# A graph network on one core: the share of node blocks that PE and POOL serve in its edge layer, and how edge weights reach the messages

## The chip, the cores and the metric

One core of a Trainium2 chip runs the whole network as one program. Times are device microseconds. The kernel before took 4041.06 us, the median of three runs (4039.64 to 4046.97).

## What is computed

There are 6250 nodes with 64 features and 200000 edges, sorted by destination. Four layers follow one another, each as x = layernorm(x + layer(x)).

```python
# layer 0: mean of the neighbours, one matrix over [h, mean]
# layer 1: twice: h = norm * segment_sum((h * norm)[src] * w, dst); mean of the three h
# layer 2: a message for every edge
x = jnp.concatenate([h[src], h[dst], e], axis=1)
m = jax.nn.relu(x @ W1 + b1) @ W2 + b2
h_new = jax.ops.segment_sum(m, dst, num_segments=h.shape[0])
# layer 3: two rounds of mean aggregation with matrices 64 -> 128 -> 64
```

Layer 2, the edge layer, is the one that cannot be done by a matrix of counts, since a relu stands on each edge. Its input splits into P[src] + Q[dst] + e * w, where P and Q are products per node (Q with b1 added) and w is the last row of W1.

## The kernel before

**Nodes and stages.** The nodes lie in 50 blocks of 125, in 10 groups of five. The stages: bounds of every node's edges are counted, with a histogram of edges by pair of blocks (`histogram`, L1672, on DVE, 34 batches of 46 columns); the 50 block matrices of counts and of weights are built and stored to DRAM (PE L1287, ScalarE L1041), with layer 0's dense sums inside (L1260); the node steps of layer 0; two weights passes for layer 1 (`weights_pass`, L1A and L1B); the edge layer (L2); two passes of layer 3 (L1328).

**Weights passes.** For each of the five blocks of a group, SP loads a matrix of 3125 KB (L697, three buffers; block 3 and block 4 of a group reuse those of blocks 0 and 1), and PE multiplies it in 100 matmuls (L1333), called a dense block below. Beside it the edges of the blocks that PE serves in the edge layer are sorted by source block. One sort: `sort_runs` on DVE (keys and one-hot comparisons), `sort_base` on PE (17 matmuls, L1428), `sort_ranks` on DVE (L2135 to L2147), then `sort_half` twice, DVE's product (L2154, L2160) and then 33 matmuls on PE (L1438), which gather local node number, local destination and three bf16 pieces of the edge weight into slots; ScalarE stores the halves to `sorted_edges`. PE, DVE and ScalarE take these steps in a written order between the dense blocks: one sort per group, the bases after dense block 0, the halves after dense blocks 3 and 4. In the second pass DVE also ends layer 1 for the group before (`finish`), and `dst_half` (L2053) makes Q.

**Edge layer.** Each group of five blocks has two served by PE (the last two) and three by POOL. The unit of order is a chunk: a block of POOL's has 33 columns of 128 edges and three chunks of 11. For each chunk:

- POOL gathers P rows by 11 indirect DMAs into one of four buffers (`gather_runs`, L931); a buffer is free when PE has collected the chunk four before.
- DVE compares the broadcast local destinations with the node numbers (`hot`, L2214, one in three chunks), PE spreads Q onto the edges (`spread`, L1475, 33 matmuls), DVE multiplies e by w (L2223) and adds PE's result from PSUM (L2227), makes the slot matrix (`slots_of`, L2234) and adds all to the gathered rows (`arrive`, L2241); ScalarE takes the relu (L1176); PE collects into the sums by destination (L1480).
- PE's own blocks, 100 slots of 128 sorted edges a group, go along in portions called units: SP broadcasts node and destination keys over 128 partitions into two tiles and then loads the three rows of edge weights (`load_unit`, L766); DVE makes one-hot matrices (L2193, L2194); PE multiplies them with the split P and Q (L1510, L1513, six matmuls a slot); ScalarE takes the relu (L1153); DVE makes slot matrices (L2205) in parts of up to six slots; PE collects (L1480).

All queues are in order. The DVE loop (L2248 and on) takes hot, unit hots, the Q half, unit slots, slots, arrive for each chunk. `split` (L556) cuts an f32 tile into three bf16 pieces: three casts and two subtractions with drains between them. At the start of the edge layer DVE splits P and then Q for all nodes.

## Time and profile before

| | |
|---|---|
| median of three runs | 4041.06 us |
| profiled execution | 4037.8 us, its span 4035.9 us |
| mean granted TensorE clock | 0.880 |
| busy: PE, DVE, ACT, POOL | 2965.3, 2213.4, 937.2, 1393.3 us |
| gathers of the edge layer (L931) | 990, 1091.0 us busy, mean 1102 ns |
| HBM read and written | 634.20 and 250.86 MB |

Busy is the time in which an engine had an instruction running. A wait is put down to the engine or transfer whose signal came last. PEclk is the clock that PE was granted, as a share of 2.4 GHz. The chain of waits follows the execution back from its end; the engines on it set the time.

### The profile page before, as it was taken

The page shows a single profiled execution, that of the slowest core. Times are in us where ns is not written, and L with a number is a line of the kernel's source. Part 1 is how long each engine was busy: PE and PEld are TensorE (multiplying, and loading weights), DVE is VectorE, ACT ScalarE, POOL GpSimd, SP SyncE. Part 2 cuts the span into 40 slices and gives each one's busy share as a digit, 9 for nine tenths or more (in the row PEclk, how much of TensorE's full clock was granted, in tenths as well). Part 3 has the DMA queues.
Part 4 walks back from the last instruction along what each step waited for, and adds up shares of the span by engine and source line. Part 5 has one row for each costly group of instructions (what it writes and reads, how often), then busy time and mean ns, then how long its engine had stood idle before and what let it go on. Part 6 is the DMA issues. An engine that isn't in the chain of part 4 may idle for free.

```text
span 4035.9 us, 119777 instructions
## 1 busy us (share of the span) xinstructions
PE 2965.3 (73%) x52730; PEld 2823.6 (70%) x52730; DVE 2213.4 (55%) x3076; ACT 937.2 (23%) x1994; POOL 1393.3 (35%) x1262
## 2 busy tenths in 40 slices
PE   0636999999995888888984655655555556489898
PEld 0635999999994878888874544555545555489898
DVE  8955777677766554455656555555545555411122
ACT  0004777777771000000000111111111111100000
POOL 5478100000000000000007777777777777600100
PEclk9999999999995999999996777777777777799999
DMA  4414787777884999999974333343333333287797
GB/s 122 83 35 128 272 289 286 269 284 273 287 288 163 402 403 391 403 391 404 400 325 114 93 92 99 99 109 92 91 100 97 104 97 99 69 346 288 261 380 312
DMA packets 334176, 891.87 MB, mean 221 GB/s; under 512 B 124164, under 2 KB 199032, under 8 KB 304088
## 3 DMA queue, kind: packets, MB, share of 16 engines
q1 hardware_dynamic: 279400, 835.28, 55.9%
q0 software_dynamic: 44480, 47.34, 5.6%
q8 instruction: 389, 6.37, 0.6%
q10 hardware_dynamic: 9792, 1.93, 0.3%
q14 instruction: 115, 0.94, 0.1%
HBM read 634.20 MB, written 250.86 MB: 219 GB/s over the span
## 4 chain that ended last, share of the span: by engine, by line
PE 32%; POOL 28%; issue 16%; DMA 15%; DVE 5%; ACT 1%; SPq 1%; POOLq 1%; DVEq 1%; ACTq 0%
POOL stream L931 27%; DMA stream<-a_weights 13%; PE ps L1287 13%; PE ps L1333 6%; PE ps L1260 5%; PE ps L1328 5%; POOL stream L909 1%; DVE junk L1615 1%; DMA a_counts<-stream 1%; ACT stream L1041 1%; DVE junk L1693 1%; DVE stream L1678 1%; PE ps L1394 1%; PE ps L1228 1%; SPq L675 0%
## 5 line engine op out<-in xcount | busy, mean ns | idle before, releaser
L931 POOL DMA_INDIRECT stream<-table,stream x990 | 1091.0, 1102 | 1998.9 <-DMA stream<-dst_run 1697.3
L1287 PE MATMUL ps<-operand_room 64*128 64x50 bf16 (+1 forms) x18750 | 635.1, 221 | 17.3 <-DVE operand_room L1860 8.0
L1475 PE MATMUL ps<-edge_room,stream 125*128 125x64 bf16 x2970 | 196.2, 242 | 609.5 <-DVE stream L2227 581.3
L1287 PEld LDWEIGHTS ps<-operand_room 64*128 64x128 bf16 x18750 | 613.8, 163 | 42.5 <-DVE operand_room L1860 8.5
L1333 PE MATMUL ps<-stream,node_room 125*64 125x125 f32 x10000 | 565.0, 273 | 92.8 <-DMA stream<-a_weights 85.6
L1475 PEld LDWEIGHTS ps<-edge_room,stream 125*128 125x128 bf16 x2970 | 185.4, 162 | 619.4 <-DVE stream L2227 416.8
L1333 PEld LDWEIGHTS ps<-stream,node_room 125*64 125x64 f32 x10000 | 542.0, 137 | 108.1 <-DMA stream<-a_weights 98.3
L1041 ACT CAST stream<-ps 128x500 bf16<-128x500 f32 (+2 forms) x700 | 431.3, 633 | 194.3 <-PE ps L1287 155.1
L1041 ACT COPY stream<-ps 128x500 f32<-128x500 f32 (+2 forms) x700 | 422.1, 619 | 0.0
L1328 PE MATMUL ps<-operand_room,stream 125*125 125x192 bf16 x3750 | 326.8, 250 | 4.4 <-POOLq L567 4.4
L1328 PEld LDWEIGHTS ps<-operand_room,stream 125*125 125x125 bf16 x3750 | 321.8, 140 | 4.6 <-POOLq L567 4.6
L2234 DVE TENSOR_TENSOR stream<-slot_f,stream 128x1375 f32<-128x1375 f32 x90 | 143.5, 1595 | 275.4 <-PE ps L1480 265.4
L1153 ACT ACTIVATE node_room<-ps 128x384 f32<-128x384 f32 (+1 forms) x180 | 83.5, 464 | 891.1 <-PE ps L1513 882.6
L1860 DVE TENSOR_TENSOR operand_room<-operand_room,node_room 128x2400 bf16<-128x2400 bf16 x200 | 280.4, 1402 | 0.0
L1853 DVE TENSOR_TENSOR operand_room<-high_iota,node_room 128x800 bf16<-128x800 bf16 x200 | 115.0, 575 | 257.0 <-PE ps L1287 256.9
L1260 PE MATMUL ps<-edge_room,stream 125*125 125x192 bf16 x2500 | 252.7, 253 | 0.5 <-ACT stream L1041 0.5
L1480 PE MATMUL ps<-stream 128*64 128x125 f32 x1980 | 227.1, 397 | 20.6 <-ACT stream L1176 20.6
L1856 DVE TENSOR_TENSOR operand_room<-low_iota,operand_room 128x2000 bf16<-128x2000 bf16 x200 | 239.1, 1195 | 0.0
L1260 PEld LDWEIGHTS ps<-edge_room,stream 125*125 125x125 bf16 x2500 | 215.1, 138 | 7.5 <-ACT stream L1041 0.7
L1480 PEld LDWEIGHTS ps<-stream 128*64 128x64 f32 x1980 | 199.0, 215 | 26.4 <-issue 21.0
L1510 PE MATMUL ps<-operand_room,node_room 125*128 125x64 bf16 x3000 | 209.9, 199 | 0.0
L1513 PE MATMUL ps<-edge_room,node_room 128*128 128x64 bf16 x3000 | 206.7, 197 | 0.0
(269 smaller groups left out, 3516.4 us busy)
## 6 DMA issues: line engine op xcount, KB each, us to landing
stream<-a_weights SPq DMA_DIRECT2D x100, 3125.0 KB, 16.7
a_weights<-stream SPq DMA_DIRECT2D x500, 312.5 KB
stream<-a_counts SPq DMA_DIRECT2D x100, 1562.5 KB, 9.1
a_counts<-stream SPq DMA_DIRECT2D x500, 156.2 KB
node_room<-sorted_edges SPq DMA_DIRECT2D x120, 352.0 KB
stream<-dst_run SPq DMA_DIRECT2D x30, 1056.0 KB, 5.8
stream<-table,stream POOLq DMA_INDIRECT x990
node_room<-sorted_edges SPq DMA_DIRECT2D x40, 256.0 KB
```

The source lines that it names most:

```text
L931: pool.indirect_dma_start(emsg[s][:, t, :], None, tables[L2][:, :], bass.IndirectOffsetOnAxis(src_t[j % 3][:, at:at + 1], 0))\
L1041: ins = act.copy(place, psum)
L1260: ins = pe.matmul(ps_low[jj % 2][0:Q, :], h_of[0:Q, h, :], parts[L0][h // PART][0:Q, h % PART, :], start=h == 0, stop=h == NPP - 1)
L1287: ins = pe.matmul(out if step == 0 else out[:, 1:2], low[s][rows_a, :, t], planes[s][rows_a, t // TI, what, :, t % TI], start=step == 0, s ...
L1328: ins = pe.matmul(ps_sum[SUM_BANK[MATRIX[k]][b]][0:Q, 0:3 * D], a[0:Q, h, :], parts[k][h // PART][0:Q, h % PART, :], start=h == 0, stop=h ...
L1333: ins = pe.matmul(ps_sum[SUM_BANK[MATRIX[k]][b]][half:half + D, 0:Q], tab_in_of(k)[0:Q, h, :], a[0:Q, h, :], start=h < 2, stop=h >= NPP - 2)
L1475: ins = pe.matmul(ps_q[:, t * D:(t + 1) * D], hot_dst[0:Q, :, at], qparts[0:Q, POOL_BLOCKS[i], v * D:(v + 1) * D], start=v == 0, stop=v == 2)
L1480: return pe.matmul(sums[half * D:(half + 1) * D, m * Q:(m + 1) * Q], rows_of, hots, start=first, stop=last)
L1510: pe.matmul(ps_unit[w % 2][:, m * D:(m + 1) * D], hot_p[c % 2][0:Q, some], pparts[0:Q, lo + m, v * D:(v + 1) * D], start=v == 0, stop=False)
L1513: ins = pe.matmul(ps_unit[w % 2][:, m * D:(m + 1) * D], hot_q[c % 2][:, some], qparts[:, PE_BLOCKS[b], v * D:(v + 1) * D], start=False, st ...
L1856: v.tensor_tensor(low[s][:, 0:Q, :], low_iota[:, 0:Q, :], lo_key[:, at].unsqueeze(1).to_broadcast([P, Q, BT]), ALU.is_equal)
L1860: v.tensor_tensor(planes[s][:, :, 1:4], planes[s][:, :, 0:1].to_broadcast(shape), w_key[:, at_w].unsqueeze(3).to_broadcast(shape), ALU.mul ...
```

## The change

PE serves three of the five blocks of a group and POOL two, so that there are 30 sorted blocks and 20 gathered ones, 60 chunks. A unit has 25 slots in five parts of five. Three sorts stand over two groups in the weights passes, in a new order. The edge weights of POOL's blocks are no longer multiplied on DVE: they are split once (`load_e`, the head of `sort_tables`, `store_e`) and stored to DRAM as three bf16 rows (`e_rows`); these rows are loaded below the one-hot rows of `hot_dst`, with w's pieces below those of Q, so that the spread's matmuls add e * w. ScalarE copies the spread's result out of PSUM. Keys of runs and units are broadcast straight into the tiles in which the one-hot matrices then take their place. Rings: hot matrices 3, unit results 3, slot matrices 5. Q is split group by group in `dst_half`. The histogram has 46 batches of 34 columns and covers three sorted blocks a group.

```diff
-    PEG = 2
+    PEG = 3
...
-                hi = min(todo[1], (lo // NPP + 1) * NPP, lo + 6)
+                hi = min(todo[1], (lo // NPP + 1) * NPP, lo + 5)
...
+    SUB = 5
+    URING = 3
+    SRING = 5
+    HRING = 3
...
-        HC = EPP // STEPS
+        HC, BATCHES = STEPS, CHUNKS
...
@@ load_edges_of_blocks (SP)
-                        for tile, of in ((src_t, src_run), (e_t, e_run), (dst_t, dst_run)):
+                        for tile, of in ((src_t, src_run), (dst_t, dst_run)):
...
-                        sp.dma_start(dst_bc[:, :], dst_run[bass.ds(start, RUN)].partition_broadcast(P))\
+                        if i >= 2:
+                            sp.wait_ge(q_done, (i - 1) * CPB)
+                        sp.dma_start(dst_bc[i % 2][0:Q, :], dst_run[bass.ds(start, RUN)].partition_broadcast(Q))\
                           .then_inc(bc_in, 16)
-                    if 0 <= c + 1 < NCH:
-                        load_unit(c + 1)
+                        sp.dma_start(hot_dst[i % 2][Q:P, :], e_rows[:, bass.ds(start, RUN)]).then_inc(bc_in, 16)
+                    if 0 <= c + 2 < NCH:
+                        load_unit(c + 2)
...
@@ load_unit (SP)
-                else:
-                    sp.wait_ge(unit_hot, u)
+                if u >= 2:
+                    sp.wait_ge(unit_hot, u - 1)
+                if u >= HRING:
+                    sp.wait_ge(unit_ps, SUB_AT[u - HRING + 1])
...
+            def load_e():
+                sp.wait_ge(dense_done, NPP)
+                sp.dma_start(e_all[:, :], e_run[0:EDGES].rearrange("(p t) -> p t", p=P)).then_inc(e_moved, 16)
+            def store_e():
+                sp.wait_ge(e_split, 1)
+                sp.dma_start(e_rows[:, 0:EDGES].rearrange("v (p t) -> p v t", p=P), e_pieces[:, :, :])\
+                  .then_inc(e_moved, 16)
...
@@ edges_act (ScalarE)
+                def copy_half(c):
+                    act.wait_ge(q_done, c + 1)
+                    if c >= 3:
+                        act.wait_ge(arrived, c - 2)
+                    act.copy(q_sb[c % 3], ps_q[:, 0:CW].rearrange("p (t d) -> p t d", d=D)).then_inc(q_used, 1)
...
@@ weights_pass (PE)
+                    def even(b):
+                        if b == 0:
+                            turn_sums()
+                            if a:
+                                sort_half(a - 1, 1)
+                            sort_base(a)
+                        if b == 1:
+                            if nodes:
+                                pe.wait_ge(base_used, a + 1)
+                            turn_rows()
+                        if b == 2:
+                            product()
+                            sort_half(a, 0)
+                            if a:
+                                sort_slots(a - 1)
+                        if b == 3:
+                            sort_half(a, 1)
+                            sort_base(a + 1)
+                    def odd(b):
+                        if b == 0:
+                            turn_sums()
+                            sort_half(a + 1, 0)
+                            sort_slots(a)
+                        if b == 1:
+                            if nodes:
+                                pe.wait_ge(slot_out, 2 * (a + 1))
+                            turn_rows()
+                            sort_half(a + 1, 1)
+                        if b == 2:
+                            product()
+                            sort_base(a + 2)
+                        if b == 4:
+                            sort_half(a + 2, 0)
+                            sort_slots(a + 1)
...
@@ edges_pe
-                            ins = pe.matmul(ps_q[:, t * D:(t + 1) * D], hot_dst[0:Q, :, at],
-                                            qparts[0:Q, POOL_BLOCKS[i], v * D:(v + 1) * D], start=v == 0, stop=v == 2)
+                            ins = pe.matmul(ps_q[:, t * D:(t + 1) * D], hots[:, :, at],
+                                            qparts[:, POOL_BLOCKS[i], v * D:(v + 1) * D], start=v == 0, stop=v == 2)
...
                     if units:
                         unit(c, 0)
+                    if 1 <= c <= NCH:
+                        collect_unit(c - 1, len(SUBS[c - 1]) - 1)
...
                     for n in range(1, units):
                         unit(c, n)
-                    for n in range(units):
-                        collect_unit(c, n)
+                        collect_unit(c, n - 1)
...
@@ dst_half (DVE)
+                to = r[0:Q] if mode == "linear" else grp(keep, g)
+                v.tensor_tensor(to, ps3(ps_o, 2 * D)[:, :, D:2 * D], row_bc(ROW_B1), ALU.add)
+                if mode == "linear":
+                    piece = [qparts[0:Q, g * GT:(g + 1) * GT, i * D:(i + 1) * D] for i in range(3)]
+                    split(v, piece, to, sq[0:Q], qparts_rdy)
...
@@ sort_tables (DVE)
+                v.wait_ge(e_moved, 16)
+                split(v, [e_pieces[:, i, :] for i in range(3)], e_all[:, :], e_all[:, :], e_split)
...
@@ weights_pass (DVE)
+                    a = (first + g) // 2 * 3
+                    if g % 2 == 0 and a and (g < GROUPS or k == L1B):
+                        sort_half(a - 1, 1)
+                    if g % 2 == 0 and g < GROUPS:
+                        sort_runs(a)
                     if g:
                         take_sums(k, g - 1, "linear")
                         finish(k, g - 1, "linear")
+                    if g % 2:
+                        sort_half(a + 1, 1)
+                        sort_runs(a + 2)
+                    elif g < GROUPS:
+                        sort_ranks(a)
+                        sort_half(a, 0)
                     if g and k == L1B:
                         dst_half(g - 1, "linear")
+                    if g % 2:
+                        sort_ranks(a + 2)
+                        sort_half(a + 2, 0)
+                    elif g < GROUPS:
+                        sort_half(a, 1)
+                        sort_runs(a + 1)
+                        sort_ranks(a + 1)
+                        sort_half(a + 1, 0)
...
@@ edges_dve
-                    v.tensor_tensor(tmp, e_t[i % 3][:, lo:lo + CHUNK].unsqueeze(2).to_broadcast([P, CHUNK, D]),
-                                    rows[:, ROW_E:ROW_E + 1, :].to_broadcast([P, CHUNK, D]), ALU.mult)
-                    v.tensor_tensor(tmp, tmp, ps_q[:, 0:CW].rearrange("p (t d) -> p t d", d=D), ALU.add)\
...
-                    v.tensor_tensor(emsg[c % MSGS], emsg[c % MSGS], etmp[c % 2], ALU.add).then_inc(arrived, 1)
+                    v.wait_ge(q_used, c + 1)
+                    v.tensor_tensor(emsg[c % MSGS], emsg[c % MSGS], q_sb[c % 3], ALU.add).then_inc(arrived, 1)
...
@@ histogram, in the counting loop (DVE)
-                if j >= 13 and j % 3 == 1:
-                    histogram((j - 13) // 3)
+                if j >= 13 and j % 2 == 1:
+                    histogram((j - 13) // 2)
```

## Rows read from the trace of the kernel before

**Rows 1.** the chain of waits of the page, shares of the span by line

```profile
POOL stream L931 27%; DMA stream<-a_weights 13%; PE ps L1287 13%; PE ps L1333 6%; PE ps L1260 5%; PE ps L1328 5%; POOL stream L909 1%; DVE junk L1615 1%; DMA a_counts<-stream 1%; ACT stream L1041 1%; DVE junk L1693 1%; DVE stream L1678 1%; PE ps L1394 1%; PE ps L1228 1%; SPq L675 0%
```

**Rows 2.** windows: us, busy PE PEld DVE ACT POOL (x), PEclk, DMA share, GB/s

```profile
1700.00:2105.00 405.00, 361.56 (x6037) 345.47 (x6039) 236.90 (x359) 32.37 (x115) 0.00 (x0) 0.99 0.97 395
2126.80:2150.90 24.10, 0.98 (x17) 1.01 (x18) 22.22 (x10) 0.00 (x0) 22.27 (x6) 0.50 0.17 51
2150.90:3519.40 1368.50, 770.02 (x13005) 709.75 (x13003) 730.54 (x913) 160.09 (x296) 1068.76 (x984) 0.73 0.37 97
```

**Rows 3.** waits of PE in the edge layer: us in total, times, longest

```profile
PE ps L1475 <- DVE stream L2227: 581.3, 89, 18.5
```

**Rows 4.** timeline: start us, us, engine line op tiles xcount [idle before <-releaser]

```profile
2717.52 1.65 DVE L2205 TENSOR_TENSOR node_room<-slot_f,stream 128x750 f32<-128x750 f32 x2
2717.76 1.51 POOL L931 DMA_INDIRECT stream<-table,stream  x1 [0.30 <-issue]
2719.57 0.94 POOL L931 DMA_INDIRECT stream<-table,stream  x1 [0.30 <-issue]
```

**Rows 5.** timeline of PE, one collect and two steps of a unit

```profile
2711.39 1.51 PE L1480 MATMUL ps<-node_room 128*64 128x125 f32 x22
2714.15 0.25 PE L1510 MATMUL ps<-operand_room,node_room 125*128 125x64 bf16 x3
2714.33 0.25 PE L1510 MATMUL ps<-operand_room,node_room 125*128 125x64 bf16 x3
```

**Rows 6.** by shape, edge layer: xcount | busy us, mean ns | idle before

```profile
L2234 DVE TENSOR_TENSOR stream<-slot_f,stream 128x1375 f32<-128x1375 f32 x90 | 143.5, 1595 | 275.4 <-PE ps L1480 265.4 <-issue 10.0
L2205 DVE TENSOR_TENSOR node_room<-slot_f,stream 128x625 f32<-128x625 f32 x80 | 64.3, 804 | 0.0
L2193 DVE TENSOR_SCALAR node_room<-node_room,node_f 125x1408 bf16<-125x1408 bf16 x80 | 47.8, 597 | 144.1 <-DMA node_room<-sorted_edges 138.6 <-issue 5.5
```

**Rows 7.** chain of waits in order of time, first weights pass

```profile
1403.16 11.38 DMA stream<-a_weights
1414.58 5.44 PE ps L1333 x97
```

**Rows 8.** timeline of DVE, one group of the second weights pass

```profile
1871.81 0.49 DVE L1955 COPY total<-ps 125x320 f32<-125x320 f32 x1 [10.56 <-PE ps L1348]
1878.33 0.38 DVE L2135 TENSOR_REDUCE operand_room<-ps 128x50 bf16<-128x100 f32 x1
1889.46 2.37 DVE L2160 TENSOR_TENSOR operand_room<-operand_room 128x4250 bf16<-128x4250 bf16 x1
1898.12 0.18 DVE L2104 TENSOR_SCALAR operand_room<-operand_room 128x33 f32<-128x33 int16 x1
1901.94 0.19 DVE L2128 CAST operand_room<-operand_room 128x34 bf16<-128x34 f32 x1
```

**Rows 9.** timeline after the build: DVE, and SP's first load of a run

```profile
1220.00 0.23 DVE L2076 CAST junk<-junk 128x128 bf16<-128x128 f32 x1
1222.99 3.49 DVE L2273 TENSOR_TENSOR node_room<-xcur,rows 125x3200 f32<-125x3200 f32 x1
1228.59 0.36 SPq L738 DMA_DIRECT2D operand_room<-packed  x1
```

**Rows 10.** groups by shape, DVE: the parts of a split of 3200 columns

```profile
L560 DVE TENSOR_TENSOR stream<-node_room,operand_room 125x3200 f32<-125x3200 f32 x1 | 3.5, 3493 | 0.1
L562 DVE CAST operand_room<-stream 125x3200 bf16<-125x3200 f32 x1 | 1.8, 1829 | 0.1
```

**Rows 11.** groups: the two operations of the histogram

```profile
L1678 DVE TENSOR_TENSOR stream<-high_iota,node_room 128x2300 bf16<-128x2300 bf16 x34 | 46.2, 1357 | 3.4 <-PE ps L1221 2.1
L1683 DVE TENSOR_TENSOR stream<-bound_s,operand_room 128x1380 bf16<-128x1380 int16 x34 | 29.6, 871 | 0.0
```

**Rows 12.** timeline of PE at the end of the second weights pass

```profile
2105.95 2.24 PE L1438 MATMUL ps<-operand_room 128*125 128x128 bf16 x33
2109.20 1.27 PE L1348 MATMUL ps<-ident,hidT 128*125 128x64 f32 x10 [1.01 <-ACTq L1140]
```

More of the change, by code:

```diff
@@ L485, in build_program @@
         slot_in = sem("slot_in")
-        unit_in = sem("unit_in")
-        unit_e = [sem(f"unit_e{s}") for s in range(2)]
+        unit_in = [sem(f"unit_in{s}") for s in range(2)]
         unit_hot = sem("unit_hot")
@@ L1171, in edges_act @@
                             take_sums(g - 1)
+                        if n == 0 and c + 2 < NCH:
+                            copy_half(c + 2)
                     if k == 0 and g and not units:
@@ L1216, in _ @@
             pe.transpose(ps_t[:, 0:D], w0[:, :], ident[0:D, 0:D]).then_inc(w0_ps, 1)
-            for m in range(STEPS):
+            for m in range(BATCHES):
                 pe.wait_ge(hist_rdy, m + 1)
@@ L1307, in build, with dense @@
                 low_dense(NPP - ITERS * JI - 1)
-            def dense(k, g, between=()):
+            def dense(k, g, between=lambda b: None):
                 what = MATRIX[k]
@@ L1335, in dense @@
                     ins.then_inc(dense_done, 1)
-                    if b < len(between):
-                        for step in between[b]:
-                            step()
+                    between(b)
             def turn(k, g, back=0):
@@ L1445, in weights_pass @@
                 for g in range(GROUPS):
-                    m = first + g
-                    between = [[] for _ in range(GT)]
-                    for b, step in enumerate(node_steps(k, g, "linear", back=1) if g else ()):
-                        between[b].append(step)
-                    if m:
-                        between[0].append(lambda: sort_slots(m - 1))
-                    between[0].append(lambda: sort_base(m))
-                    for h in range(2):
-                        between[GT - 2 + h].append(lambda h=h: sort_half(m, h))
@@ L1455, in weights_pass @@
-                    dense(k, g, between)
-                for step in node_steps(k, GROUPS - 1, "linear"):
-                    step()
-                if k == L1B:
+                    a = (first + g) // 2 * 3
+                    turn_sums, *nodes = node_steps(k, g, "linear", back=1) if g else [lambda: None]
+                    turn_rows, product = nodes or [lambda: None] * 2
+                    def even(b):
[11 more added lines that the diff above has]
+                            sort_half(a, 0)
+                            if a:
+                                sort_slots(a - 1)
+                        if b == 3:
+                            sort_half(a, 1)
+                            sort_base(a + 1)
@@ L1459, in weights_pass @@
+                    dense(k, g, odd if g % 2 else even)
+                turn_sums, *nodes = node_steps(k, GROUPS - 1, "linear")
+                turn_sums()
+                if k == L1B:
+                    turn_rows, product = nodes
+                    sort_half(NPE - 1, 1)
+                    pe.wait_ge(slot_out, 2 * (NPE - 1))
+                    turn_rows()
+                    product()
                     sort_slots(NPE - 1)
@@ L1575, in run @@
                         with pe.Fori(1, GROUPS) as g:
-                            dense(k, g, [[step] for step in node_steps(k, g, mode, back=1)])
+                            steps = node_steps(k, g, mode, back=1)
+                            dense(k, g, lambda b: steps[b]() if b < len(steps) else None)
                         for step in node_steps(k, GROUPS - 1, mode):
@@ L1718, in _ @@
             v.tensor_copy(n(end_i), n(tmpn)).then_inc(end_rdy, 1)
-            for m in range(13, 28):
+            for m in range(19, 38):
                 histogram(m)
@@ L1732, in _ @@
             v.drain()
-            for m in range(28, STEPS):
+            for m in range(38, BATCHES):
                 histogram(m)
             v.tensor_reduce(n(gmax), n(deg), AX.X, ALU.max)
-            v.wait_ge(hist_used, STEPS)
+            v.wait_ge(hist_used, BATCHES)
             v.tensor_copy(hist_f[0:2 * NPP, :], ps_hist[0:2 * NPP, 0:2 * NB])
```

219 lines of the change are left out of this document (114 added, 105 removed).

## The prediction

> **What bounds the kernel now.** I read the chain of waits first, by line [rows 1]: the gathers of POOL hold 27% of the span and the loads of the weight matrices 13%; the rest lies in stages that the change leaves alone. Then the windows of the stages [rows 2]. In the edge layer (2126.8 to 3519.4 us, 1392.6 us) POOL issues 990 gathers without a wait for anybody. After the first 24.1 us, in which DVE splits its tables, 984 gathers take 1368.5 us, that is 1.391 us each, 15.30 us for a chunk of 11. PE runs at a mean clock of 0.73 there and waits 581.3 us in 89 waits, 6.5 us a chunk [rows 3]. So POOL alone sets this stage. In the second weights pass the DMA is busy 0.97 of the time at 395 GB/s, and DVE 237 of 405 us: the matrix loads set it, 40.5 us for a group of five blocks [rows 2]. The steps of that loading are in [rows 7]: a load issued when a dense block ends lands 11.4 us later, and its own dense block takes 5.6 us. The first load of a group waits for dense block 3 of the group before, since it takes its buffer. From one landing to the other that is 17.0 us for two loads, where the other three take (40.5 - 17.0) / 3 = 7.8 us each. So whatever delays dense block 3 delays the next group by the same.
>
> **Edge layer, POOL.** 30 blocks of three chunks become 20: 60 chunks, 660 gathers. A gather takes 0.94 us and 0.30 us of gap when DVE leaves it alone [rows 4], 13.7 us a chunk. The other 1.6 us of the 15.3 come from DVE: a gather that started at 2717.76 ran to 2719.27, just behind DVE's pair of comparisons (2717.52 to 2719.17) [rows 4]. DVE's work on a chunk changes. Taken away: the two operations of the edge weights (L2223, L2227). Added: units grow from 100/9 = 11.1 to 25 slots. Their slot matrices are five comparisons of 625 columns, up to 0.80 us each [rows 6], together 3.6 to 4.0 us in place of 1.65 [rows 4]. The two hot comparisons go from 1408 to 3200 columns, 0.60 us [rows 6] to between 1.0 and 1.4 us each. The comparison of 1375 columns (1.6 us) and arrive stay. The operations of over 0.7 us thus grow from about 4 to 8 us a chunk. If their toll grows with them, 1.6 becomes 3.2 us; if the gaps between the five short ones let POOL through, it stays at 2. I take 2.9: a chunk of 16.6 us, 1.509 us a gather. At the start only one of two splits of 3200 columns (each near 12.5 us: two of 3.49 and three of 1.83 [rows 10]) still stands beside POOL. In the window with both, six gathers took 24.1 us [rows 2]; I give the first two 9 us. Sum: 9 + 658 x 1.509 = 1002 us, against 1392.6: **-391 us**. Bounds: 15.3 us a chunk (-469), and 19.1 (the first rival, -247).
>
> **Edge layer, the others.** They must stay under 16.6 us a chunk. PE: 15.3 - 6.5 = 8.8 us of work and small gaps now. Added are 13.9 slots, each six unit matmuls (0.18 us, start to start in [rows 5]) and two passes of a collect (1.51 / 22 x 2 = 0.14 us [rows 5]): 4.4 us at 2.4 GHz, 8.9 us at 1.2 GHz; and some six more waits, 1 us. That is 14.2 to 18.7 us. The clock was 0.73 of full with 6.5 us idle in a chunk and 0.99 in the weights pass with PE busy 362 of 405 us [rows 2]; with the idle time gone from 6.5 to about 2 us I expect it near full for most of a chunk, so PE stays just under POOL. DVE: 4 + 2.4 + 1.6 + 0.9 + 0.5 for hot, and the group's finish (some 9 us over six chunks), 11 us. ScalarE takes the copy of 704 columns, beside POOL, 5 us a chunk in all; hidden, 0.8 us a chunk if it were not. The wait of SP for the units of three chunks before leaves the loads of a unit one chunk of lead; bytes per chunk rise to some 2.3 MB (keys 25 x 256 B x 125 x 2 = 1.6, a third of a run's broadcast 0.35, gathers 0.36), 140 GB/s against the 395 that the weights pass reaches [rows 2]: hidden. Behind SP's wait stand only the next runs, which are three deep. Rings of 3, 5 and 3 take waits away that PE did not sit in; nothing.
>
> **Weights passes.** 30 blocks are sorted beside 20 groups in place of 20. One sort costs DVE 13.5 us from the ranks to the end of half 0, 2.4 for half 1 and 4.0 for the runs [rows 8], 20 us. DVE per two groups of the second pass: 3 x 20, two finishes of 6.5 [rows 8], two dst_half of 0.6 that now split 320 columns as well (five operations of 0.5 and their drains, 2.9): 80 of 81 us. I followed the order by hand, with t = 0 where dense block 0 of an even group ends, 5.6 us a dense block, 2.2 us a half and 1.3 us a turn on PE [rows 7, 12]. Second pass, even group: base at 4.4, finish to 7.8, half 0 ready at 21.3 where PE arrives at 17.6; dense block 3 ends at 29.3, the next matrix lands at 40.7, its dense block ends at 46.3 in place of 40.4. Odd group: half 0 of the second sort at 45.9, just in time; product at 65.5, dst_half to 69.5, half 0 of the third sort ready at 83.0 where PE stands at 77.6; next dense block 0 ends at 91.0 in place of 80.7. So 10.3 us a pair; the last pair loses 6.2 of them before its last dense block ends: 4 x 10.3 + 6.2 = 47.5 us. In the first pass the sums and finish are four operations of 0.5 us, 2.1 us, and dst_half is missing: half 0 ready at 17.9 where PE is at 15.6, dense block 3 at 25.9 in place of 24; the pair closes at 83.6 in place of 80.4: 5 x 3.2 = 16 us. Edge weights moved between the passes: one split of 64 columns and three copies, 4 us, of which 3 show. Between the last dense block's end (2106.0) and the last sums (2110.5, the end of the turn) stands one half of 2.2 us now [rows 12]; then a half 0 that comes 5.4 us late, its 2.2 us, and on DVE half 1 of 2.4 us: 10.0 in place of 4.5, and the 16.3 us from there to POOL's first gather [rows 2, 12] stay. Sum 47.5 + 16 + 3 + 5.5: **+72 us**. Bounds: 15 (the slack of DVE hides all but the tail) and 110 (the waits come out half as long again).
>
> **Before them.** The histogram has 46 batches of 34 columns for 34 of 46: 1.36 and 0.87 us [rows 11] become 1.00 and 0.86. Nineteen in DVE's counting loop cost 35.3 us where 13 cost 29.0; eight at the end 14.9 where six cost 13.4; those between lie beside the loads of below. **+8 us**. The edge weights' own split now stands ahead of the sort's tables and of L2273, with which the node steps begin at 1222.99 [rows 9]. It needs e_all, whose load SP issues where it issued the first run, at 1228.6 [rows 9], since it stands behind the stores of the matrices: landed at some 1233 (an estimate, 0.8 MB at half the rate of [rows 2]), split of 1564 columns 6.5 us (half of [rows 10]), then the 3.0 us from L2076 to L2273 [rows 9]: L2273 at 1243. **+20 us**, on the path, for the first dense block of the weights waits for these node steps. Bounds 12 and 25.
>
> **Sum.** -391 + 72 + 8 + 20 = -291. The profiled execution took 4037.8 us, span 4035.9, and would take 3747; the median of the runs (4041.06) stands 3 us above it, so **3750 us**.
>
> **Rivals.**
> (1) POOL is held for nearly all of DVE's long operations. In the stretch of the splits DVE was busy 22.2 us and POOL made six gathers, one in 3.7 to 4 us [rows 2]. With some 8.2 us of such work a chunk: 2.2 gathers in it and the other 8.8 at 1.245, 19.1 us, edge layer 1146 us, total 3894. For it: [rows 2]. Against it: the operations there are of 3.49 and 1.83 us with no wait between, and the pair in [rows 4] cost 0.6 us only. A rule of the Trainium skill speaks against the change here (SBUF — State Buffer, section SBUF: two separate sides): VectorE and GpSimd share a pair of ports as an exclusive lock, held for a whole instruction, and meanwhile a GpSimd DMA cannot write its descriptors. By that rule, at its strictest, this rival's time holds; [rows 4] agree in kind, since the gather ended behind the comparisons, and not in size. PE at a clock that stays near 0.73 gives about the same, 18 to 19 us a chunk.
> (2) Neither toll grows: POOL keeps 15.3 us a chunk and DMA hides the sorts but for some 27 us. 3750 - 78 - 45 = 3627. For it: DVE is busy 237 of 405 us only; against: half 0 is needed at fixed places.
> (3) Slower. PE falls to 1.2 GHz for the whole stage and becomes its bound: 8.8 x 0.73 / 0.5 = 12.8, and 8.9 and 1 us on top, 22.7 us a chunk, 1362 us; with the +100 us elsewhere 4110. It decides from (1392.6 - 100) / 60 = 21.5 us a chunk. Against it: a PE that works without a pause showed 0.99 [rows 2].
> (4) The change doesn't do what it says: a further block with more than 128 edges from one source block would send all to the other branch, several ms. 200000 edges over 2500 pairs are 80 each, spread 9: under 1 in 100.
>
> **Chances.** Forecast (3700 to 3810) 0.50; (1) 0.22; (2) 0.22; (3) 0.04; rest 0.02. The range leaves out the far halves of (1) and (2): 3640 to 3880. A difference of 0.2%, 8 us, is what can be told from none. Faster 0.94, same 0.01, slower 0.05.
>
> **What would show it.** The gathers 660, mean 1.2 us and gap 0.30; edge layer near 1000 us; PEclk there 0.85 or more, PE waits for DVE or ScalarE still some us a chunk. Wrong if PE waits for nothing and POOL for s_done. Weights passes: pairs of 83 to 84 and of 91 us, DVE's L2160 with waits of dense blocks behind it. L2273 near 1251 us.

## The result, and the profile after

The changed kernel ("after" below) takes 3944.9 us (median; 3942.1 to 3949.1), the kernel before ("before") 4040.4 beside it: a ratio of 0.9759 with a 95% interval of 0.9744 to 0.9774. It is faster, by 95 us. Forecast were 3750 us with a range of 3640 to 3880, so the time lies outside, 195 us above the forecast.

The chain of waits of the changed kernel, by line, to be held against [rows 1]:

```profile
PE ps L1341 14%; DMA stream<-sorted_edges 13%; PE ps L1387 7%; PE ps L1314 6%; PE ps L1382 5%; DMA stream<-a_weights 4%; PE ps L1568 3%; PE ps L1490 2%; DVE operand_room L2232 2%; POOL stream L938 1%; DMA node_room<-sorted_edges 1%; PE ps L1597 1%; PE ps L1600 1%; DVE operand_room L2249 1%; DVEq L2257 1%
```

POOL's gathers (27% before) are gone from the chain. In their place stands the load of PE's keys, `stream<-sorted_edges` and `node_room<-sorted_edges`, 14%. The forecast had called this load hidden.

The windows (columns as in [rows 2]): the second weights pass, then the edge layer from POOL's first gather to the end of its last:

```profile
1735.00:2225.00 490.00, 417.20 (x6708) 402.66 (x6703) 371.00 (x561) 38.28 (x139) 0.00 (x0) 0.92 0.84 340
2248.79:3395.89 1147.10, 821.69 (x14784) 733.28 (x14784) 555.59 (x681) 215.84 (x430) 750.76 (x660) 0.83 0.44 124
```

The 660 gathers are there and take 1.138 us each (forecast 1.2), but POOL is busy only 751 of 1147 us. A chunk takes 1147.1 / 60 = 19.1 us. The waits of the edge layer (us in total, times, longest) show in what order the engines wait:

```profile
DVE stream L2299 <- DMA stream<-sorted_edges: 453.0, 39, 20.2
POOL stream L960 <- PE ps L1568: 206.8, 37, 15.3
...
PE ps L1568 <- DVE node_room L2310: 191.7, 29, 19.9
```

POOL waits for PE's collect, PE for DVE's comparisons, and DVE for the keys: DVE's 453 us (and 99.5 for the third buffer) are the source. In the chain in order of time (start, us, what), these loads are the longest pieces:

```profile
2656.15 20.92 DMA stream<-sorted_edges
2681.62 21.10 DMA stream<-sorted_edges
...
2725.25 15.07 DMA stream<-sorted_edges
```

Between the first two stand 4.6 us, between the last two 22.5 us, mostly steps of DVE. Of the chain from 2640 to 2760 us the loads are 48%.

The table (us) sets the profiled execution of after (span 3945.5) against that of before (4035.9) and the forecast; the last column is the experiment cut112, below.

| stretch | before | forecast | after | cut112 |
|---|---|---|---|---|
| to POOL's first gather | 2126.8 | +100 | +122.0 | +123.3 |
| first to last gather | 1392.6 | -391 | -245.5 | -404.1 |
| from there to the end | 516.5 | 0 | +33.1 | -9.3 |
| span | 4035.9 | -291 | -90.4 | -290.1 |

### The profile page after: what moved, and what is told of

The parts are those of the page before. It is cut to its first block, busy times and chain, and to the rows that moved or that the text cites. A ratio compares the mean times of both kernels' runs of the same rounds, so it can differ in the third digit from the quotient of the medians.

```text
span 3945.5 us, 126344 instructions
## 1 busy us (share of the span) xinstructions
PE 3128.3 (79%) x55930; PEld 2953.8 (75%) x55930; DVE 2267.7 (57%) x3200; ACT 1009.3 (26%) x2184; POOL 1048.2 (27%) x932
## 4 chain that ended last, share of the span: by engine, by line
PE 43%; DMA 20%; DVE 16%; issue 12%; DVEq 3%; POOL 2%; SPq 2%; ACT 1%; POOLq 1%; ACTq 0%
PE ps L1341 14%; DMA stream<-sorted_edges 13%; PE ps L1387 7%; PE ps L1314 6%; PE ps L1382 5%; DMA stream<-a_weights 4%; PE ps L1568 3%; PE ps L1490 2%; DVE operand_room L2232 2%; POOL stream L938 1%; DMA node_room<-sorted_edges 1%; PE ps L1597 1%; PE ps L1600 1%; DVE operand_room L2249 1%; DVEq L2257 1%
## 5 line engine op out<-in xcount | busy, mean ns | idle before, releaser
L960 POOL DMA_INDIRECT stream<-table,stream x660 | 750.8, 1138 | 2207.1 <-DMA stream<-dst_run 1810.8
L1387 PEld LDWEIGHTS ps<-stream,node_room 125*64 125x64 f32 x10000 | 553.1, 140 | 57.4 <-DMA stream<-a_weights 45.2
L1568 PE MATMUL ps<-node_room 128*64 128x125 f32 x2400 | 248.5, 321 | 273.4 <-DVE node_room L2310 202.6
L1568 PEld LDWEIGHTS ps<-node_room 128*64 128x64 f32 x2400 | 182.5, 160 | 289.5 <-DVE node_room L2310 206.4
L1382 PE MATMUL ps<-operand_room,stream 125*125 125x192 bf16 x3750 | 320.1, 247 | 4.4 <-POOLq L577 4.4
L1197 ACT ACTIVATE node_room<-ps 128x320 f32<-128x320 f32 x300 | 131.4, 438 | 745.5 <-PE ps L1600 737.2
L1382 PEld LDWEIGHTS ps<-operand_room,stream 125*125 125x125 bf16 x3750 | 314.5, 137 | 4.7 <-POOLq L577 4.7
L2299 DVE TENSOR_SCALAR stream<-stream,node_f 125x3200 bf16<-125x3200 bf16 x40 | 42.5, 1064 | 464.3 <-DMA stream<-sorted_edges 464.3
L1597 PE MATMUL ps<-operand_room,stream 125*128 125x64 bf16 x3000 | 223.7, 203 | 7.8 <-DVEq L2300 7.8
L1600 PE MATMUL ps<-edge_room,stream 128*128 128x64 bf16 x3000 | 221.6, 203 | 0.0
L1490 PE MATMUL ps<-operand_room 128*125 128x128 bf16 x1980 | 153.4, 243 | 72.4 <-DVEq L2257 72.4
L1597 PEld LDWEIGHTS ps<-operand_room,stream 125*128 125x128 bf16 x3000 | 171.6, 105 | 47.5 <-issue 47.5
```

The source lines that it names most:

```text
L960: pool.indirect_dma_start(emsg[s][:, t, :], None, tables[L2][:, :], bass.IndirectOffsetOnAxis(src_t[j % 3][:, at:at + 1], 0))\
L1382: ins = pe.matmul(ps_sum[SUM_BANK[MATRIX[k]][b]][0:Q, 0:3 * D], a[0:Q, h, :], parts[k][h // PART][0:Q, h % PART, :], start=h == 0, stop=h ...
L1387: ins = pe.matmul(ps_sum[SUM_BANK[MATRIX[k]][b]][half:half + D, 0:Q], tab_in_of(k)[0:Q, h, :], a[0:Q, h, :], start=h < 2, stop=h >= NPP - 2)
L1490: ins = pe.matmul(ps_half, half_vals[:, t // 2, :, :, t % 2].rearrange("p i s -> p (i s)"), hot_rank[:, t // 2, :, t % 2], start=t == 0, s ...
L1568: return pe.matmul(sums[half * D:(half + 1) * D, m * Q:(m + 1) * Q], rows_of, hots, start=first, stop=last)
L1597: pe.matmul(ps_unit[w % URING][:, m * D:(m + 1) * D], hot_p[c % HRING][0:Q, some], pparts[0:Q, lo + m, v * D:(v + 1) * D], start=v == 0, s ...
```

## The experiments

Times are medians. Where nothing else is said, the kernel before took 4039 to 4047 us on the chip of the run. The theories: **A**, the broadcasts of keys to 125 partitions run on only five DMA engines; **B**, SP issues them late and in bunches; **C**, the DMA system as a whole is full. What speaks for A: in the trace of after, the packets of a key row are of 6400 bytes and take 257 ns in the mean, and five packets of the queue are in flight at once for some 61% of the stage, more than five for some 6%. Before, where the same loads went to 128 partitions, up to 16 were in flight. 125 = 25 x 5: a load of 125 rows is then 25 rows on each of five, 6.4 us (25 x 257 ns), a pair 12.9.

The Trainium skill (DMA: Bandwidth & Descriptors, section "Why a DMA increments its semaphore by 16 and not by 1") states the rule: a transfer is spread over the largest number of engines up to 16 that divides the outermost dimension (of a size above 1) of both its source and its destination. It would give five for 125 partitions, and the trace agrees, with its five packets in flight.

**The keys' loads cut at partition 112 (cut112), at 115 (cut115), at 100 (cut100).**

```
+    CUT = 112        # 115, 100
     for tile, i in ((hot_q, 0), (hot_p, 1)):
-        sp.dma_start(tile[u % HRING][0:Q, place]... .partition_broadcast(Q))
+        for r0, r1 in ((0, CUT), (CUT, Q)):
+            sp.dma_start(tile[u % HRING][r0:r1, place]... .partition_broadcast(r1 - r0))
...  (the same for dst_bc, and the counts of the two waits in DVE)
```

> The changed kernel, with each broadcast of keys to 125 partitions (the two of a unit, and that of a run) issued as two loads, partitions 0 to 111 and 112 to 124. Theory A (few engines): in the changed kernel these loads show five packets of 6400 bytes in flight at once, 257 ns each, since 125 rows are dealt out in equal shares only to five engines, 25 rows each; 112 rows go to sixteen, 7 each, and 13 to thirteen, 1 each. So 8 rows an engine for 25: the pair of key loads takes some 4 us for 12.9, DVE no longer waits for them, and the stage goes by POOL: 11 gathers of 1.14 and 0.30 us = 15.8 us a chunk for 19.6, edge layer 950 to 1000 us for 1178, total 3725 to 3775 us. Theory B (SP issues the loads too late, behind its waits, whatever their rate): landing shortens but DVE still waits some 10 us a chunk, total 3880 to 3945. Theory C (the DMA system as a whole is short of bandwidth beside the gathers): nothing moves, 3945 or more.

> Control to the cut at 112: the same number of loads of nearly the same size, cut at partition 115 (115 rows go to five engines, 23 each, and 10 rows to ten, 1 each: 24 rows on the busiest engine for 25). Theory A: within 10 us of the changed kernel, 3935 to 3955, five packets in flight as before. If it is the cutting into more loads that helps, and not the engines, it gives the same time as the cut at 112.

> A dose between: cut at partition 100. 100 rows go to ten engines, 10 each, and 25 to five, 5 each: 15 rows on the busiest engine, 7.7 us for the pair of key loads. Theory A: the pair and the wait behind it are shorter than a chunk of POOL, which then sets most chunks: 16 to 17.5 us a chunk, total 3740 to 3830. Theory B: like the cut at 112, whatever that gives.

| kernel | us | ratio to before | rows on the busiest engine (worked out) | first to last gather, us |
|---|---|---|---|---|
| after | 3944.9 | 0.9759 [0.9744, 0.9774] | 25 | 1147.1 |
| cut115 | 3939.4 | 0.9742 [0.9724, 0.9760] | 24 | 1143.3 |
| cut100 | 3791.2 | 0.9371 [0.9346, 0.9396] | 15 | 1003.6 |
| cut112 | 3750.4 | 0.9279 [0.9262, 0.9297] | 8 | 988.5 |

The rows on the busiest engine take it that both parts of a load start on the same engines; the trace does not number the engines. What it shows is how many packets of the queue are in flight together most often: 5 in after, 5 in cut115, 10 in cut100, 16 in cut112. The control at 115 has the same number of loads as the cut at 112, with three rows moved from one to the other, and gives nothing; the cut at 112 gives 194 us. So it is the engines and not the cutting, and C falls: cut112 moves 145 GB/s where after moves 124. All three came as theory A had it. The stage and DVE's waits for keys in cut112:

```profile
2250.11:3238.63 988.52, 807.72 (x15330) 720.15 (x15331) 588.15 (x719) 222.49 (x445) 787.66 (x660) 0.89 0.63 145
```

```profile
POOL stream L963 <- issue: 200.9, 659, 0.3
...
DVE stream L2302 <- DMA stream<-sorted_edges: 65.6, 12, 12.4
```

POOL waits for nobody, 0.30 us of gap ahead of 659 gathers, and stands on the chain again:

```profile
POOL stream L963 21%; PE ps L1344 13%; PE ps L1390 8%; PE ps L1385 6%; PE ps L1317 5%; DMA stream<-a_weights 4%; PE ps L1493 3%; DVE operand_room L2235 2%; DMA a_counts<-stream 2%; POOL stream L941 2%; ACT stream L1073 1%; SPq L686 1%; DVE operand_room L2252 1%; DVEq L2260 1%; DVE junk L1707 1%
```

**The reverse, on the kernel before (before125).**

```
-    sp.dma_start(tile[:, place]... .partition_broadcast(P))
+    for r0, r1 in ((0, Q), (Q, P)):
+        sp.dma_start(tile[r0:r1, place]... .partition_broadcast(r1 - r0))
...  (the same for dst_bc)
```

> The kernel before, with its broadcasts to 128 partitions cut into 125 and 3: same bytes, but five engines and three. Theory A: its units are of 11 slots (2816 bytes a row, 160 ns a packet): 25 rows an engine make 4 us a load, 8 us for the two, beside a chunk of 22.8 us that POOL sets; DVE waits longer for keys and POOL does not: same time as before, 4040, within 10 us. So five engines alone cost nothing until the units grow. If it is slower by over 20 us, the lead of the loads was short already.

4291.6 us, 252 more than before: my expectation of no change failed. The stage takes 1655.8 us:

```profile
2130.30:3786.15 1655.85, 773.62 (x12975) 713.25 (x12976) 749.33 (x923) 162.14 (x295) 1088.74 (x990) 0.68 0.35 81
```

and its chain is the loads again, 8 us for a pair, 16 where a run's broadcast stands ahead of it:

```profile
2612.43 8.23 DMA node_room<-sorted_edges
...
2635.52 16.13 DMA node_room<-sorted_edges
```

The waits show the same. The first line is of before, the others of before125, where POOL now waits for PE:

```profile
DVE node_room L2193 <- DMA node_room<-sorted_edges: 204.7, 29, 9.4
```

```profile
DVE node_room L2195 <- DMA node_room<-sorted_edges: 577.5, 61, 19.2
...
POOL stream L933 <- PE ps L1482: 280.0, 47, 9.7
```

I had set 8 us against POOL's chunk of 15.3 us (22.8 in the expectation, which was wrong) as if they ran side by side. They don't: the load waits until DVE has used its buffer, and DVE, in its order, stands at the next comparison until the load has landed, and only then does what PE and POOL wait for. Landing and DVE's and PE's steps of a chunk add up. So the five engines alone cost 252 us, even with the small units of before. (Its 2816-byte packets took 126 ns in the mean, for the 160 of the expectation.)

**SP's order (keys3; cut112_keys3 with the cut).** What speaks for B: SP's own waits in after (between 2300 and 3300 us), and what it issues:

```profile
SPq L798 <- DVE node_room L2310: 504.4, 26, 26.4
```

```profile
2648.27 0.72 SPq L803 DMA_DIRECT2D node_room<-sorted_edges  x2
2649.03 0.31 SPq L805 DMA_DIRECT2D node_room<-sorted_edges  x1
2655.38 0.73 SPq L803 DMA_DIRECT2D stream<-sorted_edges  x2
...
2658.44 0.31 SPq L773 DMA_DIRECT2D stream<-dst_run  x1
...
2680.88 0.70 SPq L803 DMA_DIRECT2D stream<-sorted_edges  x2
```

Two units and a run's broadcast are issued within 11 us (2 x 12.9 + 8.4 = 34 us of work for five engines), then nothing for 22 us. This fits the 21 us in which the first two loads shown above landed, where 12.9 are worked out for a pair.

```
-    slot_key = [... for _ in range(2)]
+    slot_key = [... for _ in range(3)]
-    if b:
-        sp.wait_ge(unit_slots, LAST_SUB[b - 1] - (NPP // SUB - 1) + 1)
+    if b >= 2:
+        sp.wait_ge(unit_slots, LAST_SUB[b - 2] - (NPP // SUB - 1) + 1)
```

> The changed kernel with its five engines kept, and three buffers for the slot keys in place of two. SP's wait in front of the slot keys of a new block goes (504 us in 26 waits between 2300 and 3300 us): with two buffers the load of every second unit stood behind the first slot comparison of the unit two before it, which DVE makes only after the hot comparisons of the next unit; so two units and a run's broadcast were issued together, and nothing in the meantime. Theory A+B (rate and bunching together make the 19.6 us): the five engines have 1.6 MB of keys and 0.35 MB of a run's broadcast a chunk, 15.9 us at the 123 GB/s of this stage; spread evenly they go beside POOL's 15.8, a chunk of 16.5 to 18, total 3770 to 3860 us. Theory A alone (only the rate counts): 3925 to 3945, as without it.

> The cut at 112 with the three buffers for slot keys on top. With sixteen engines the chain of this stage is POOL's gathers one behind the other, and DVE waits for keys only 48 us in 10 waits between 2300 and 3100 us: the earlier issue is hidden, 3740 to 3752 us against 3750 for the cut alone. If SP's waits still set chunks there, 3720 or less.

keys3: 3853.8 us, 91 less than after, as theory A+B had it; the stage takes 1053.3 us, 17.6 a chunk, and DVE still waits 382.5 us for keys. With the cut as well: 3753.9 against 3750.4, nothing. So B is real and holds only on top of A: 91 of the 195 us come back with a better order on five engines, all with sixteen.

**Keys or run's broadcast (cut_run, cut_units, cut_units_again).** One of the two edits of cut112 each.

> Only the broadcast of a run (1.03 MB, one in three chunks) cut at 112; the loads of the units' keys stay on five engines, 1.6 MB a chunk. Five engines then have 12.9 us of keys a chunk and 2.8 us of the run's broadcast every third chunk, where they had 12.9 and 8.5. Theory A+B: the landing of the keys stays on the chain, and the chunk with the broadcast is some 6 us shorter, 2 us a chunk: 120 us less than the changed kernel at most, 3825 to 3880 us. If the units' keys alone make the loss, 3920 to 3940; if the run's broadcast alone, 3750 to 3765.

> Only the loads of a unit's keys cut at 112; the broadcast of a run (1.03 MB, one in three chunks) stays on five engines. It takes 8.5 us there and stands in the same rings: keys behind it on those five engines wait for it. Theory A: one chunk in three is late by up to 8.5 us less the slack of the load (some 8 us between a landing of 4 us and its use in a chunk of 16.4): 0 to 5 us each, 3750 to 3850 us, likeliest 3765. If the broadcast of the run was the one that counted, it stays near 3900.

> The fourth corner: only the units' keys cut at 112, the run's broadcast on five engines, on a chip that can be compared with the others. On the other chip its ratio to the kernel before was 0.956 where the cut of both with the late split and the new order had 0.9467; taking 30 us off for those two leaves some 10 us for the run's broadcast. So 3755 to 3770 us, against 3750 with both cut and 3906 with the run's alone: the keys are the loss, and the run's broadcast counts (39 us) only where the keys already fill the five engines.

cut_run took 3906.2 us, 39 less than after; I expected 65 to 120. cut_units_again took 3738.9, ratio 0.9251 [0.9230, 0.9272], where I expected 3755 to 3770; it is no slower than with both cut (0.9279 [0.9262, 0.9297]). The two ran on different chips, and of the 15 us between their profiled executions 12.6 lie ahead of POOL's first gather, where the kernels are the same; the stage takes 982.5 us for 988.5. So the units' keys on five engines are the whole loss: the run's broadcast there costs nothing once they are off, and 39 us while they are on. cut_units itself ran on a slower chip, on which the kernel before took 4388.6 us (ratio 0.9560), so its expected time can't be tested.

**The toll of DVE on POOL (noslots, nohots, nodve),** all on cut112. The toll is the time by which DVE's operations lengthen POOL's gathers. These kernels leave out most of the slot comparisons of PE's units, of the hot comparisons, or of both.

```
-    some = slice(0, sum(hi - lo for b, lo, hi in SUBS[u]) * P)
+    some = slice(0, P)                                  # nohots, nodve
+    wide = Q if w < SRING else 5                        # noslots, nodve
-    v.tensor_tensor(unit_slot[...][:, 0:hi - lo, :], slot_f[:, 1:Q + 1]...
+    v.tensor_tensor(unit_slot[...][:, 0:hi - lo, 0:wide], slot_f[:, 1:wide + 1]...   # noslots, nodve
```

> The cut at 112, with the slot comparisons of PE's units cut from 625 to 25 columns (behind the first five of them; leaves out that part of the slot matrices). The prediction's term of the toll: POOL's gathers are lengthened by DVE's operations beside them. In the run of the cut, the gathers have 0.94 us with no DVE operation beside them and 1.24 with one of these, and 2.8 us a chunk in all are above 0.94. Leaving four microseconds of DVE out of a chunk gives 0.7 to 0.9 us a chunk, 40 to 55 us, 3695 to 3710 us. If the gathers are long for another reason (busy DMA rings), 3745 to 3755.

> The cut at 112, with the two hot comparisons of a unit cut from 3200 to 128 columns (leaves out the rest of the comparison). They take 2.1 us of DVE a chunk, half of what the slot comparisons take, but the gathers beside them ran for 1.54 to 1.67 us where 0.94 is the shortest. If their toll is larger per microsecond of DVE, 1.1 us a chunk: 50 to 65 us, 3685 to 3700 us. If the toll goes by DVE's busy time, half of what leaving the slots out gives, 20 to 27 us, 3723 to 3730.

> The cut at 112, with both comparisons of a unit cut short: hots from 3200 to 128 columns, slots from 625 to 25 (leaves out the rest of both). The gathers were busy for 27 to 34 us less without the slots and 54 to 61 us less without the hots, whatever the total did there. If both tolls are DVE's and add, the 660 gathers take 695 to 705 us in place of 788, a chunk of POOL 11 x (1.06 + 0.30) = 15.0 us for 16.4; PE's 13.4 us of busy time stay below it. Total 3665 to 3690 us. If PE's own chain comes up in POOL's place, 3700 to 3750.

noslots (4262.3 us) and nohots (4335.7) ran on the chip of cut_units. Their totals can't be used: on that chip PE stands still for 313 to 437 us of this stage without a wait that the profile shows (19 to 51 in cut112 and the kernels made from it that ran on the usual chips). The kernel `best` (below) shows it too, and why is not settled. What can be read is how long the gathers were, in `best`, noslots, nohots and, on a usual chip, nodve:

```profile
L963 POOL DMA_INDIRECT stream<-table,stream x660 | 780.5, 1183 | 2358.7 <-DMA stream<-dst_run 1801.3
```

```profile
L963 POOL DMA_INDIRECT stream<-table,stream x660 | 753.2, 1141 | 2508.0 <-DMA stream<-dst_run 1861.0 <-PE ps L1571 463.1 <-issue 183.9
```

```profile
L963 POOL DMA_INDIRECT stream<-table,stream x660 | 726.7, 1101 | 2600.6 <-DMA stream<-dst_run 1846.7 <-PE ps L1571 570.1 <-issue 183.9
```

```profile
L963 POOL DMA_INDIRECT stream<-table,stream x660 | 710.8, 1077 | 2005.7 <-DMA stream<-dst_run 1804.9 <-issue 200.2 <-PE ps L1571 0.6
```

Against `best`, the gathers are busy 27 us less without the slots (40 to 55 were expected of the total) and 54 less without the hots (50 to 65). Without both, in nodve, they are busy 77 us less than cut112's 787.7; the stage takes 911.6 us, 77 less, and the total is 3673.0, 77 less and within the expected 3665 to 3690. What DVE no longer does shortens the gathers, and the gathers are the time. DVE was busy 174 us less in this stage in noslots and 89 us less in nohots than in `best`: a microsecond of slot comparison costs POOL 0.16 us, one of hot comparison 0.60. The two add up to 81 us, near the 77 of nodve.

By the Trainium skill (SBUF — State Buffer, section SBUF: two separate sides) DVE, when it starts first, holds the port pair that it shares with POOL for a whole instruction in its faster (2-port) modes, while an operation with two inputs holds it only against POOL's reads. These tolls agree in their order (bfloat16 against one value per partition dear, two-input comparison cheap); neither is 1, and no run shows in which mode an operation ran. The prediction told this rule without the difference between the two kinds.

**The two smaller steps (cut112_late, cut112_order),** both on cut112.

```
     def sort_tables():                       # late: the split of the edge weights leaves this place
-        v.wait_ge(e_moved, 16)
-        split(v, [e_pieces[:, i, :] ...], e_all[:, :], e_all[:, :], e_split)
...
     if g % 2:                                # ... and stands ahead of the third sort's ranks
+        if k == L1A and g == 1: ... split(...)
         sort_ranks(a + 2)
```

```
     if b == 1:                               # order, PE, odd groups
         turn_rows(); sort_half(a + 1, 1)
+        pe.wait_ge(turned_sb, ...); sort_base(a + 2)
     if b == 2:
         product()
-        sort_base(a + 2)
...  (order, DVE: dst_half(g - 1) behind the sorts of a group)
```

> The cut at 112, with the split of the edge weights moved from in front of the node steps into the first weights pass, where DVE waits 7.5 us for PE in front of the ranks of the third block (group 1). The split itself is 6.5 us of DVE and waited 14.7 us for its load. By the prediction's step of +20 us at this place: the node steps begin 20 us earlier and 15 to 21 us are gained, 3730 to 3736 us. Rival: the first weights pass is held by the matrix loads from its start, and takes it back: 3745 or more.

> The cut at 112, with two steps of the weights passes in another order: PE makes the base of a pair's third sort behind half 1 of the second, one dense block earlier, and DVE takes the dst half of a group last. In odd groups of the second pass PE waits 4.7 us for half 0 of the third sort (5 groups), in even groups 4.4 to 5.8 us for half 0 of the first. If those waits are DVE's order, as the prediction's step has it, the odd groups lose none and the even ones keep theirs less up to nothing: 15 to 30 us less in the second pass, 3720 to 3735 us. Rival: the matrix loads (DMA busy 0.85 there) end last as soon as the waits go: 3742 or more.

late: 3729.6, ratio 0.9222 [0.9204, 0.9241]: 21 us, as expected. order: 3741.7, ratio 0.9253 [0.9240, 0.9266]: 9 us, where 15 to 30 were expected. In the second pass the waits for DVE's halves fell from 57.8 us in cut112 to 29.5 (both by PE's weight loads), and PE's waits for the matrices rose from 15.3 to 30.0, as the rival had it:

```profile
PE ps L1390 <- DMA stream<-a_weights: 30.0, 11, 3.8
PEld ps L1493 <- DVEq L2262: 29.5, 11, 4.9
```

**Together (all_three, best, best_units).**

> The cut at 112, the late split, the new order of the weights passes and the three buffers for slot keys. On a chip where the kernel before takes 4040 us: 3750 - 21 - 9 = 3720 us (3712 to 3728), ratio 0.919 to 0.923, since the three stages don't touch each other; the slot keys add nothing (POOL's gathers are the chain). If the first weights pass takes one of the two back, 3730.

> The cut at 112, the late split of the edge weights and the new order of the weights passes together: three gains in three stages that don't touch each other, 194, 21 and 9 us, so 3720 us (3712 to 3728). If the late split and the new order both only move waits within the first weights pass, 3730.

> Only the units' keys cut at 112, with the late split and the new order of the weights passes: the version that the other runs point to. 3739 - 21 - 9 = 3709 us (3700 to 3720). If the 10 us between the two cuts (3739 against 3750) are a difference of chips, 3718 to 3722, like the kernel with both cut.

all_three: 3720.5 us, as expected, ratio 0.9209 [0.9196, 0.9223]: the best version measured, 321 us below before and 224 below the change. best (without the third slot-key buffer) and best_units (without the run's cut) ran where before took 4388.6 and 4392.8: 0.9467 [0.9440, 0.9494] and 0.9478 [0.9464, 0.9492], so no difference between the two can be told; their expected times can't be tested there.

## Why the prediction was wrong, step by step

- **DMA of the edge layer: the step that failed.** It read: "bytes per chunk rise to some 2.3 MB ..., 140 GB/s against the 395 that the weights pass reaches [rows 2]: hidden". The bytes were right; the 395 are those of loads that 16 engines share. The key loads go to 125 partitions in place of 128, five engines take them, and the stage moves 124 GB/s, all told: DVE waited 453 and 99.5 us for them, and the cut at 112 alone brings 194 us back. "The wait of SP ... leaves the loads of a unit one chunk of lead" failed with it: every second unit waits for a slot comparison behind the next unit's hot comparisons. The full diff showed both: `partition_broadcast(P)` became `(Q)`, and the wait went from `LAST_SUB[b - 2]` to `LAST_SUB[b - 1]`. None of the rivals was a load.
- **POOL at 16.6 us a chunk.** Right once the loads are off the chain: cut112 has 988.5 us between first and last gather for 1002, gathers of 1.193 us and a gap of 0.30 for 1.2 and 0.30, and the total is 3750.4. That this is no chance agreement shows in nodve, which took 77 us of gathers away and 77 of the stage. Of the toll's 2.9 us a chunk, the runs show 11 x (1.193 - 0.94) = 2.8.
- **PE just under POOL.** Right: 808 us busy in 988.5 at a clock of 0.89 ("0.85 or more"). In after it is 0.83. The sign said to be decisive ("wrong if PE waits for nothing and POOL for s_done") was half there: POOL waited for PE's collect (206.8 us) and PE waited as well, since both stood behind DVE and the load.
- **Behind the last gather.** Counted as unchanged; it was +33.1 us in after, as PE's last units came late: layer 3's first products (L1382) start 50.3 us behind the last gather, 16.5 in before. In cut112 (15.4) the stretch is -9.3; the 8 us that are left were not placed.
- **Setup and node steps, +8 and +20.** L2273 was forecast near 1251, and its counterpart began at 1254.6 in after and at 1252.4 in cut112: +31.6 and +29.4 for the forecast +28. The load of the edge weights, put at 1233 + 8, landed at 1244.7: that is the 3.6 us by which the +28 was short in after. The kernel cut112_late gave 21 us back.
- **First weights pass, +16.** From the first dense block (1297.9 before, 1329.5 after) to the last sums +21.
- **Second weights pass, 47.5 + 3 + 5.5 = 56.** It was +70, 14 us more. Steady pairs of groups take 95.5 us for the forecast 91.0 (81 to 82 before). The times inside a pair (the last one of cut112, whose passes are those of after) came out as worked out, counted from the end of dense block 0: half 0 ready at 21.4 for 21.3, the next matrix at 41.0 for 40.7, half 0 of the third sort at 83.4 for 83.0. What I mis-sized is what PE does after it has waited:

```profile
2163.73 3.78 PE L1490 MATMUL ps<-operand_room 128*125 128x128 bf16 x33 [4.39 <-DVEq L2257]
...
2173.05 2.25 PE L1490 MATMUL ps<-operand_room 128*125 128x128 bf16 x33
```

  The same 33 products take 3.78 us behind a wait of 4.39 us, and 2.25 later; the granted clock is 0.50 of full (1.2 GHz) in the first stretch and 1.00 in the second:

```profile
2163.80:2166.60 2.80, 2.80 (x27) 2.80 (x28) 2.41 (x5) 0.00 (x0) 0.00 (x0) 0.50 0.03 6
2173.10:2175.20 2.10, 2.10 (x37) 2.10 (x36) 1.09 (x4) 0.26 (x1) 0.00 (x0) 1.00 0.79 198
```

  Two such halves a pair are 3 of the 4.5 us; I could not place the rest.
- **The sum.** -404 + 123 - 9 = -290 in cut112 against -291: errors of -13, +23 and -9 cancel. The true miss of the forecast, taken apart from the loads, is some 20 us in the weights passes.
- **Rivals.** (1) gave 3894 by another mechanism, a chunk of 19.1 us; the chunk of after is 19.1 as well, but its gathers are short and wait. It has the size and not the cause. (2), (3) and (4) did not come.

## What to carry to other kernels

A load's speed goes by the number of DMA engines that its outermost dimension lets it have: when a diff changes 128 partitions to 125, work out the landing anew (25 rows on each of five engines for 8 on each of sixteen), and cut it at a multiple of 16. Before a transfer is called hidden, compare its landing with the time between its issue and its use in the order of the queues, not with the period of the stage; an in-order engine that waits for it adds it to all that it does after. Price a wait put in front of TensorE at the wait and at the slower clock behind it.

## What the runs showed of the hardware that I had not expected

- On five engines a 6400-byte packet takes 257 ns in the mean, 25 GB/s an engine; where up to ten are in flight (cut100) 337 ns, and up to sixteen (cut112) 394 ns, 16 GB/s. So the sixteen together are some twice as fast, not three times (an estimate from these means). Why is open: in cut112 the few packets with under five in flight take as long (421 ns).
- The toll of DVE's operations on POOL's gathers is 0.60 us per microsecond for a comparison of bfloat16 with one value per partition, and 0.16 for a two-input comparison in float32.
- Chips differ: the kernel before takes 4039 to 4047 us on most, and 4388.6 and 4392.8 on two. The gain of the changed kernels is smaller there. In the profiles from there PE has 307 to 437 us of time between its matmuls in the edge layer for which no wait is recorded, and 113 to 146 us ahead of it, where cut112 has 51 and 68; in noslots and nohots, with less work on DVE, it was more (383 and 437). This stays open.
